# All low parts of P by GpSimd, the rows in six loads, and a new order of work in a fused graph network

## The reference

```python
scores = jnp.einsum('bhqd,bhkd->bhqk', q, k) / jnp.sqrt(HD)
scores = scores + beta * adj_e
scores = jnp.where(adj_e > 0, scores, -9000000000000000.0)
out = jnp.einsum('bhqk,bhkd->bhqd', softmax(scores), v)
```

## Time and profile before

| | us |
|---|---|
| median of 3 runs | 2803.11 (2800.51 to 2803.31) |
| the profiled execution | 2813.78 |
| its span, first to last instruction | 2812.0 |
| TensorE busy | 2675.4 (95%) |
| VectorE busy | 2423.5 (86%) |
| ScalarE busy | 1811.9 (64%) |
| GpSimd busy | 1748.1 (62%) |

### The profile page before, as it was taken

One profiled execution on the slowest core, in us unless ns is written; L12 is line 12 of the kernel. 1 busy time (PEld: TensorE's weight loads), 2 busy tenths in 40 slices (PEclk: granted clock), 3 DMA queues, 4 the chain that ended last, 5 costly groups with the idle time before them and its releaser, 6 DMA issues.

```text
span 2812.0 us, 92245 instructions
## 1 busy us (share of the span) xinstructions
PE 2675.4 (95%) x34240; PEld 1988.6 (71%) x34240; DVE 2423.5 (86%) x8566; ACT 1811.9 (64%) x4885; POOL 1748.1 (62%) x2827
## 2 busy tenths in 40 slices
PE   5899998999999999999999999999999999989996
PEld 4667766777777777777777777777777777767764
DVE  7789888888888888888898888888888888888876
ACT  6546667566666666666676666666666666666546
POOL 3376665666666666666666666666666666654675
PEclk9799999999999999999999999999999999999997
DMA  7634444443454544444544454455455444454325
GB/s 175 137 71 82 82 82 85 78 80 72 87 87 78 86 85 79 88 86 78 85 89 78 81 91 82 78 90 83 80 87 88 78 86 74 70 100 81 58 41 97
DMA packets 804132, 238.89 MB, mean 85 GB/s; under 512 B 771560, under 2 KB 803440, under 8 KB 803440
## 3 DMA queue, kind: packets, MB, share of 16 engines
q1 hardware_dynamic: 795808, 218.25, 44.8%
q10 hardware_dynamic: 7888, 14.75, 1.8%
HBM read 31.54 MB, written 12.58 MB: 16 GB/s over the span
## 4 chain that ended last, share of the span: by engine, by line
PE 68%; DVE 15%; DMA 9%; issue 3%; SPq 2%; POOL 2%; ACT 1%; DVEq 0%; POOLq 0%; ACTq 0%
PE bank L850 9%; PE bank L851 9%; PE bank L852 9%; DMA turned<-flat 8%; PE bank L838 7%; PE bank L840 7%; PE bank L839 7%; PE bank L887 3%; PE bank L937 3%; PE bank L944 2%; PE bank L872 2%; PE bank L945 2%; PE bank L874 2%; PE bank L873 2%; SPq L600 2%
## 5 line engine op out<-in xcount | busy, mean ns | idle before, releaser
L838 PE MATMUL bank<-turned,w_hi 128*128 128x128 f16 x3960 | 707.9, 221 | 13.4 <-DMA turned<-flat 10.5
L840 PE MATMUL bank<-turned,w_lo 128*128 128x128 f16 x3960 | 707.0, 221 | 0.0
L839 PE MATMUL bank<-turned,w_hi 128*128 128x128 f16 x3960 | 706.9, 221 | 0.0
L850 PE MATMUL bank<-w_hi,turned 128*128 128x384 f16 x1815 | 596.4, 329 | 16.1 <-DMA turned<-flat 14.6
L851 PE MATMUL bank<-w_lo,turned 128*128 128x384 f16 x1815 | 595.6, 328 | 0.0
L852 PE MATMUL bank<-w_hi,turned 128*128 128x384 f16 x1815 | 595.2, 328 | 0.0
L759 ACT ACTIVATE ab<-bank 128x384 f16<-128x384 f32 (+1 forms) x660 | 319.9, 485 | 352.1 <-PE bank L840 190.2
L768 ACT ACTIVATE score<-score,small 128x128 f32<-128x128 f32 x1320 | 430.7, 392 | 58.4 <-DVE small L1040 36.1
L838 PEld LDWEIGHTS bank<-turned,w_hi 128*128 128x128 f16 x3960 | 390.6, 99 | 36.2 <-DMA turned<-flat 13.1
L839 PEld LDWEIGHTS bank<-turned,w_hi 128*128 128x128 f16 x3960 | 391.0, 99 | 10.6 <-issue 4.0
L840 PEld LDWEIGHTS bank<-turned,w_lo 128*128 128x128 f16 x3960 | 391.3, 99 | 0.0
(11 more groups left out here) (218 smaller groups left out, 7833.8 us busy)
## 6 DMA issues: line engine op xcount, KB each, us to landing
turned<-flat SPq DMA_TRANSPOSE x825, 2.8
last_unit<-w_dram ACTq DMA_DIRECT2D x19, 576.0 KB, 4.5
x<-x_dram SPq DMA_DIRECT2D x55, 192.0 KB, 2.3
out_dram<-score SPq DMA_DIRECT2D x55, 192.0 KB, 2.0
adj<-adj_dram SPq DMA_DIRECT2D x55, 64.0 KB, 2.3
last_unit<-last_unit SPq DMA_TRANSPOSE x135, 2.9
rows<-rows_dram ACTq DMA_DIRECT2D x1, 1920.0 KB, 10.2
last_unit<-x_dram SPq DMA_DIRECT2D x9, 192.0 KB, 2.3
```

Of the source, the lines that this page charges most:

```text
L838: pe.matmul(dst, lhsT=w_hi[:, w, k, cols], rhs=t_hi[u][:, k, :], start=(k == 0), stop=False)
L839: pe.matmul(dst, lhsT=w_hi[:, w, k, cols], rhs=t_lo[u][:, k, :], start=False, stop=False)
L840: last = pe.matmul(dst, lhsT=w_lo[:, w, k, cols], rhs=t_hi[u][:, k, :], start=False, stop=(k == DT - 1 and w not in BIAS_OF))
L850: pe.matmul(dst, lhsT=t_hi[u][:, k, :], rhs=w_hi[:, w, k, :], start=(k == 0), stop=False)
```

## The change

Three things are done.

1. The part `scores_lo` of VectorE is gone. GpSimd's part `scores`, which made the low parts of P for layer 3, now makes them for layer 0 too, with the same instruction. SyncE's transposes and VectorE's next scores wait for GpSimd's signal in both layers.
2. The 18 rows are put in another order in the tile and loaded in six pieces of three rows (`PIECE`). Each piece has a part of ScalarE after which it may be issued (`ROWS_AFTER`), and the first user of each row waits for its own piece.
3. `PERIOD`, `SHIFTED` and all dates in `PARTS` are new, so the order of parts on every engine is new. The planner's charge for TensorE after a gap is replaced by one that follows how busy TensorE was.

```diff
-ROW_OF = {5: 6, 8: 7, **{w: 3 + w for w in range(9, 15)}}
-GAIN_ROW = (0, 2, 8, 10)
+X_BIAS = (0, 1)
+ROW_OF = {5: 2, 8: 5, 9: 8, 10: 9, 11: 10, 12: 11, 13: 14, 14: 15}
+GAIN_ROW = (3, 6, 12, 16)
+
+PIECE = 3
...
-PERIOD = 41.981
+PERIOD = 41.639
...
+ROWS_AFTER = (((SCALAR, "scores", 0),), ((SCALAR, "scores", 2),), ((SCALAR, "norm", 0),), ((SCALAR, "project", 3),), ((SCALAR, "turn", 2),), ((SCALAR, "project", 6),))
...
-    (VECTOR, "scores_lo", 3): (220.776, 0.441, 0.728, ((SCALAR, "scores", 3),), ()),
+    (POOL, "scores", 3): (453.758, 0.920, 1.167, ((SCALAR, "scores", 3),), ()),
...
-        **{(SCALAR, "load_rows", k): (FIRST + n + 0.3, 0.0, 0.5, 8.0, ((SCALAR, "weight", WEIGHT_ORDER[n]),))
-           for k, n in enumerate(ROWS_AFTER)}}
+        **{(SCALAR, "load_rows", k): (FIRST + k + 0.3, 0.0, 0.5, 4.5, ROWS_AFTER[k]) for k in range(NR // PIECE)}}
...
-            if now - last_busy > COLD_AFTER:
-                busy, until = busy + min(busy, COLD), until + min(busy, COLD)
+            if last_busy > 0 and now > last_busy:
+                used *= math.exp(-(now - last_busy) / CLOCK_SPAN)
+            clock = min(1.0, max(0.45, 0.25 + 0.8 * used))
+            slower = busy / clock - busy
+            busy, until = busy + slower, until + slower
+            used = 1.0 - (1.0 - used) * math.exp(-busy / CLOCK_SPAN)
...
             def scores(i, s):
-                sp.wait_ge(*(mixed_out.at(i, "low p", s) if s < HG else low_made.at(i, "p", s)))
+                sp.wait_ge(*low_made.at(i, "p", s))
...
-                if (w, i) == first(POOL, "bias", 5, 8):
-                    pool.wait_ge(rows_loaded[0], 16)
-                if (w, i) == first(POOL, "bias", *range(9, 15)):
-                    pool.wait_ge(rows_loaded[1], 16)
+                if (w, i) == first(POOL, "bias", w):
+                    pool.wait_ge(rows_loaded[ROW_OF[w] // PIECE], 16)
...
             def load_rows(i, k):
-                part = slice(0, ROWS_SPLIT) if k == 0 else slice(ROWS_SPLIT, NR)
+                part = slice(PIECE * k, PIECE * k + PIECE)
...
-                    dve.wait_ge(*(mixed_out.at(i, "low p", s - 1) if s < HG else low_made.at(i, "p", s - 1)))
+                    dve.wait_ge(*low_made.at(i, "p", s - 1))
...
-            def scores_lo(i, s):
-                u = i % UNITS
-                dve.wait_ge(*cast.at(i, "p", s))
-                dve.tensor_tensor(flat[u][:, 1, :], score_at[u], flat[u][:, 0, :], ALU.subtract).then_inc(mixed_out.of(i), 1)
...
-                if (k, i) == first(VECTOR, "inner", 0, 1):
-                    dve.wait_ge(rows_loaded[0], 16)
-                if (k, i) == first(VECTOR, "inner", 2, 3):
-                    dve.wait_ge(rows_loaded[1], 16)
+                if (k, i) == first(VECTOR, "inner", k):
+                    dve.wait_ge(rows_loaded[GAIN_ROW[k] // PIECE], 16)
```

More of the change, by code:

```diff
@@ L1 @@
+import math
 import numpy as np
@@ L55 @@
 PARTS = {
     (PE, "turn_adj", 0): (0.000, 0.120, 0.380, ((VECTOR, "scores", 3),), ()),
[L57 to L67, removed]
@@ new lines @@
+    (VECTOR, "gain", 1): (117.533, 0.916, 1.240, ((POOL, "inner", 1),), ()),
+    (SCALAR, "turn_adj", 0): (156.469, 0.156, 0.426, ((PE, "turn_adj", 0),), ()),
+    (VECTOR, "delta_di", 1): (256.521, 0.206, 0.503, ((SCALAR, "u_di", 1),), ()),
+    (POOL, "bias", 11): (264.983, 0.920, 1.200, ((SCALAR, "project", 11),), ()),
+    (VECTOR, "scores", 3): (307.742, 0.629, 0.470, ((PE, "scores", 3), (POOL, "scores", 2)), ()),
+    (SYNC, "load", 0): (311.863, 0.900, 3.290, (), ((VECTOR, "residual", 3),)),
@@ new lines @@
+    (VECTOR, "project", 7): (412.783, 0.463, 0.741, ((SCALAR, "project", 7),), ()),
+    (VECTOR, "scores", 1): (423.681, 0.628, 0.469, ((PE, "scores", 1), (POOL, "scores", 0)), ()),
+    (SCALAR, "turn", 4): (430.331, 0.412, 0.707, ((VECTOR, "gain", 2),), ()),
+    (VECTOR, "u_gcn", 1): (437.585, 0.647, 0.867, ((PE, "u_gcn", 1), (POOL, "turn_adj", 0)), ()),
+    (VECTOR, "masks", 0): (437.700, 0.516, 0.800, ((SYNC, "load", 0),), ()),
+    (SCALAR, "scores", 3): (442.930, 1.493, 1.852, ((VECTOR, "scores", 3), (SYNC, "scores", 2)), ()),
@@ new lines @@
+    (VECTOR, "scores", 2): (523.840, 0.628, 0.469, ((PE, "scores", 2), (POOL, "scores", 1)), ()),
+    (PE, "attend", 1): (527.450, 0.234, 0.454, ((SYNC, "scores", 1),), ()),
+    (VECTOR, "gain", 3): (528.681, 0.525, 0.810, ((POOL, "inner", 3),), ()),
+    (POOL, "residual", 0): (529.013, 1.134, 1.446, ((VECTOR, "residual", 0),), ()),
+    (PE, "project", 0): (531.345, 1.685, 1.865, ((SYNC, "turn", 0),), ()),
+    (SCALAR, "project", 8): (534.156, 0.370, 0.661, ((PE, "project", 8),), ()),
+    (SCALAR, "attend", 2): (534.198, 0.133, 0.422, ((PE, "attend", 2),), ()),
@@ new lines @@
+    (VECTOR, "project", 4): (689.418, 0.466, 0.745, ((SCALAR, "project", 4),), ()),
+    (PE, "turn_delta", 1): (689.990, 0.120, 0.380, ((VECTOR, "delta_di", 1),), ()),
+    (POOL, "bias", 5): (691.516, 0.920, 1.200, ((SCALAR, "project", 5),), ()),
+    (VECTOR, "residual", 2): (695.314, 1.212, 1.565, ((VECTOR, "gain", 3),), ()),
+    (POOL, "bias", 10): (695.336, 0.920, 1.200, ((SCALAR, "project", 10),), ()),
+    (SCALAR, "scores", 2): (699.824, 1.490, 1.849, ((VECTOR, "scores", 2), (SYNC, "scores", 1)), ()),
@@ new lines @@
+    (SCALAR, "attend", 5): (821.339, 0.132, 0.421, ((PE, "attend", 5),), ()),
+    (SCALAR, "scores", 5): (823.447, 1.491, 1.850, ((VECTOR, "scores", 5), (SYNC, "scores", 4)), ()),
+    (VECTOR, "gain", 2): (827.718, 0.525, 0.810, ((POOL, "inner", 2),), ()),
+    (VECTOR, "scores", 5): (829.261, 1.214, 1.622, ((PE, "scores", 5), (POOL, "scores", 4)), ()),
+    (SCALAR, "norm", 3): (834.473, 0.597, 0.944, ((POOL, "residual", 3),), ()),
+    (SCALAR, "project", 14): (836.041, 0.371, 0.662, ((PE, "project", 14),), ()),
```

374 lines of the change are left out of this document (175 added, 199 removed).

## The result

The changed kernel takes 2787.62 us (median of 6 runs, 2781.49 to 2791.25); the kernel before, run beside it, 2803.24 (6 runs, 2800.51 to 2809.33). The ratio is 0.9942, 95% interval 0.9929 to 0.9955: 15.6 us or 0.6% faster, where the forecast was 28.5.

A forecast was written before the change was run, and what follows sets the result against it. TensorE was taken as the bound, with only its idle time and slow clock to win. The terms -10.4 - 6.7 - 9.0 - 2.4 gave -28.5 us, from median 2803.11 to 2774.6 us, range 2750 to 2808.

The forecast's parts named there:

- 600 to 2400, -9.0: Long middle stretch: TensorE's waits for VectorE and for transposes of what it made shrink by 36%, -9.0 us.
- 200 to 600, -6.7: Stretch from 200 to 600 us: TensorE's waits for VectorE and transposes shrink by 36%, -6.7 us.
- 2400 to the end, -2.4 and 0: 2400 to 2740: waits for VectorE and transposes shrink, GpSimd's grow, -2.4 us; 2740 to 2812, only layer 3 left: 0.
- more is won: Rival, chance 0.15: both ramps become like the middle and half the head's clock loss goes; -53 us, 2750.
- Head, -10.4: First 200 us: VectorE's waits, rows, clock and GpSimd's queue together, -10.4 us.
- VectorE's waits, -6.6: Head: without 24 low parts VectorE is less busy from 20 to 100, so TensorE's 12.8 us of waits halve, -6.6.
- Rows, -3.9: Head: six smaller loads replace the long one behind which a transpose takes 10.24 us, winning TensorE's 3.9 us wait.
- Clock, -3.9: Head: the 0.89 clock costs 17.0 us; the share of idle time won, 10.5 of 45.5, takes back 3.9.
- GpSimd's queue, +4.0: Head: graph 0's second-group low part stands behind four GpSimd additions needing the first rows, delaying transposes and TensorE, +4.0 us.
- Slower, the seven places: Rival, chance 0.13: later low parts from GpSimd hold graphs' buffers longer, +27 us less the head's 10.4, 2820.
- a mark of the forecast that failed: Sign of being right: SyncE's waits for layer 0's low parts below 1.2 us each.
- VectorE near 2279 us, GpSimd near 1984: Sign of being right: whole-run busy time near 2279 us or below for VectorE, near 1984 for GpSimd.

The follow-up runs named there:

- the pair near the medians: e7 and e8, standing for the kernel before and the changed kernel but for their rows' loads; profiled executions 2807.4 and 2789.4 us.
- e9: Kernel before, frozen order, layer 0's low parts moved to GpSimd and each mask one part earlier in VectorE's list; 2792.79 us, ratio 0.9968.
- e7: Kernel before, order frozen, only the rows loaded in six pieces as in the change; 2803.22 us, ratio 1.0009.
- second pair: e7 and e8, standing for the kernel before and the changed kernel but for their rows' loads; 2803.22 and 2783.57 us.
- e8: Changed kernel, order frozen, only the rows loaded in two pieces again as before; 2783.57 us, ratio to before 0.9936.
- e4: Kernel before in its own order, layer 0's low parts left out of the computation; 2776.83 us, ratio 0.9907.
- e5: Kernel before, order frozen, only layer 0's low parts moved from VectorE to GpSimd; 2821.06 us, ratio 1.0065.
- e10: Changed kernel with each mask one part earlier in VectorE's list; 2811.62 us, ratio to before 1.0035.
- e12: Kernel before, low parts on VectorE, only each mask one part earlier in VectorE's list; 2808.31 us, ratio 1.0025.
- e11: Changed kernel, order frozen, layer 0's low parts left out of the computation; 2778.06 us, ratio to before 0.9909.
- e6: Changed kernel, order frozen, only layer 0's low parts put back on VectorE; 2837.78 us, ratio 1.0127.

## Why the prediction was right, and where it was wrong

Direction and range held (2787.6 in 2750 to 2808); the sum was 28.5 and the runs show 15.6.

- **600 to 2400, -9.0.** The profiled pair shows 7.5 us of idle time less, the pair near the medians 0.2 more. Half of the mechanism held: TensorE's waits for transposes fell from 16.4 to 5.4 us, but in the old order they did not with the move alone (`L931` in e9 9.8, the same row 10.9 in e7). Its waits for VectorE, which were to shrink by 36%, grew from 8.6 to 12.8, by a new place to be late at (`L1075`, 7.7 us). The size was read from an execution whose 29.3 us of idle time was high for this kernel (24.1 in e7). The rule's input was off as well: VectorE's busy over idle time fell to 5.55 (1525.19 and 274.81) and not to 4.94, since a part of the subtractions' time overlaps their neighbours'.
- **200 to 600, -6.7.** Idle time 5.7 less (4.5 in the second pair), and the clock there from 0.98 or 0.99 to 1.00, which no term held. The size was about right, its reason not: e9 has the relief without the new order, and no gain here.
- **2400 to the end, -2.4 and 0.** Undersized: 5.0 us less idle time (41.5 to 36.5), 7.8 in the second pair, and some clock. This is a part of the rival "more is won", which I had put aside because no row spoke for better ramps.
- **Head, -10.4.** The step that failed. *VectorE's waits, -6.6:* it is busy 51.04 of 80 us from 20 to 100 in place of 57.68, more than the 44.5 I had counted on (the stretch held 19 low parts, 11.18 us, and not 24), and TensorE waits 19.6 us for it in the head instead of 12.8. *Rows, -3.9:* no gain, by e7 and e8; the other end, nothing won, was right and my choice wrong. "DMA: Bandwidth & Descriptors" of the Trainium skill, section "Issuing engines are not separate DMA queues", has all transfers interleave on the same 16 engines; the trace agrees in that the transposes are slow at other places instead (8.04 and 7.26 us in place of 10.24). *Clock, -3.9:* 0.89 to 0.90 in the first stretch and 0.85 to 0.81 from 20 to 100. *GpSimd's queue, +4.0:* GpSimd waited 2.44 us for the first rows and not 12.11; the second group's cast ended at 31.54 us and its low part began at 32.59, behind the additions, so 1.05 us late and not 4.0.
- **Slower, the seven places.** It did not happen: SyncE's wait for a place went from 57.0 us to 3.0. Its opposite was a mark of the forecast that failed: SyncE's waits for the low parts are 1.98 us, not under 1.2. The transposes that follow hold TensorE less than before all the same: a long wait of the queue was here no delay of what it feeds. So the 0.94 us of the earlier trace rows was no measure of GpSimd's answer; it was the mean of 35 waits, where 171 low parts were made.
- **VectorE near 2279 us, GpSimd near 1984.** 2307.9 and 1953.8. VectorE's 29 us above the forecast are not collisions: e4, with no low parts of layer 0 at all, reads 2305.8. The forecast took 144 us of instructions off the busy time, where 117.7 was their share of it. The 5 us given to collisions were not too few: the mask's two instructions took 73.5 us in all before (22.03 and 51.45) and take 77.5 now (26.55 and 50.91). Their place decides more than their sum, as e5 shows against e9: 0.76 us per graph ahead of what TensorE needs cost 28 us.
- The sum was set against one execution, 10.7 us over its median, and the gain was sized by that execution's idle time. A part of what I meant to win was that execution's own.
- That the result fell inside the range is in part luck: the head's 10.4 did not come, and 9.8 us of TensorE's busy time (13.4 in the profiled pair) did, for which the sum had only the head's clock, 3.9.

## What to carry to other kernels

When work moves between VectorE and GpSimd, look at what runs beside it at each end: one 128x128 instruction that stretched by 0.76 us in the wrong place turned a gain of 8.6 us into a loss of 18.6, and moving it by one part brought the gain back. What an engine is relieved of is read from a run without the instructions (here 117.7 us), not from the sum of their times (144). Where a planner sets the order, an edit and its order are one change: test an edit in a frozen order, since an order planned from foreign dates cost 110 to 175 us here. A wait put ahead of a part can cost what that part feeds, however short the instruction behind it (e10).

## What was not expected of the hardware

A `tensor_scalar` of 128x128 f32 on VectorE takes 217 to 220 ns (e7, e12), 350 (e9) or 976 (e5), each of them steady over 29 or 30 periods. The first is what it takes when VectorE does not wait; the other two are that of GpSimd's instruction still to run, 0.27 and 0.89 us, and 0.08 more. Which of the two engines pays changed between two kernels in which both start within 0.02 us of each other. Read to the nanosecond over all kernels of this case, the recorded starts lie on two sides of a border: where GpSimd's 128x384 instruction starts 12 to 16 ns ahead of this one, VectorE went through in 108 of 111 meetings (under 400 ns; nearly all of them in before, e4 and e7), and where it starts 17 to 20 ns ahead, VectorE waited in 42 of 43 (37 of them in e5). What sets the distance of the two starts in a given order stays open.

The clock from 200 to 600 is 1.00 in the changed kernel, e8, e10, e11 and e6, and 0.98 or 0.99 in before, e7, e9 and e12. TensorE's idle time there does not explain it: e6 has 21.0 us and 1.00, before 20.4 and 0.99. Why it goes with the new order stays open.
